# Layernorm, banded attention and a mixture of experts in one kernel: bulk loads issued in ACT's queue, roots by the Sqrt table, k copied out one exponent earlier

## What is computed

```
h   = x + attention(layernorm(x))          # 32 query heads, 8 key/value heads, width 64
out = h + experts(layernorm(h))            # 8 experts, hidden width 1024, top 2, capacity 640

attention: q, k, v = xn @ W_qkv; rotary tables on q and k
           scores = q k^T / 8, -inf where 0 <= q_pos - k_pos < 64
           softmax over the keys and one sink logit per head; times v; @ W_out
layernorm: (x - mean) / sqrt(var + 1e-5)
experts:   gates = softmax(xn2 @ gating_w); top 2; rows scattered to expert slots;
           relu(rows @ w1 + b1) @ w2 + b2; weighted and added back
```

## Time and profile before

| | us |
|---|---|
| median of 3 runs | 1170.53 (1166.02 to 1171.97) |
| the profiled execution, device time | 1165.65 |
| its span in the trace | 1163.8 |
| PE busy in the span | 1047.7 (90%) |
| DVE busy | 891.1 (77%) |
| POOL busy | 709.1 (61%) |
| ACT busy | 642.4 (55%) |

### The profile page before, as it was taken

One profiled execution on the slowest core, in us unless ns is written; L12 is line 12 of the kernel. 1 busy time (PEld: TensorE's weight loads), 2 busy tenths in 40 slices (PEclk: granted clock), 3 DMA queues, 4 the chain that ended last, 5 costly groups with the idle time before them and its releaser, 6 DMA issues. The chain is left out here.

```text
span 1163.8 us, 32636 instructions
## 1 busy us (share of the span) xinstructions
PE 1047.7 (90%) x13260; PEld 760.2 (65%) x13260; DVE 891.1 (77%) x1936; ACT 642.4 (55%) x1597; POOL 709.1 (61%) x586
## 2 busy tenths in 40 slices
PE   4797998998899999989999998999883799999995
PEld 3364665565565666656566665666552799999995
DVE  7999888897898998979999997999973444444442
ACT  2556665565655666565566656656643344444551
POOL 5555565667556686766577675668723266655662
PEclk9898999999999999989999999999996799999998
DMA  3443433343322333232233323233422344344431
GB/s 98 128 124 110 121 107 105 105 114 108 87 75 84 90 93 87 74 103 76 77 111 95 96 75 90 73 88 102 125 68 95 119 100 94 89 109 107 105 103 19
DMA packets 115398, 111.45 MB, mean 96 GB/s; under 512 B 35216, under 2 KB 103888, under 8 KB 115120
## 3 DMA queue, kind: packets, MB, share of 16 engines
q1 hardware_dynamic: 107952, 100.81, 29.6%
q0 software_dynamic: 7296, 8.55, 4.4%
HBM read 74.17 MB, written 21.83 MB: 82 GB/s over the span
## 5 line engine op out<-in xcount | busy, mean ns | idle before, releaser
L778 ACT ACTIVATE probs_ring<-probs_ring,neg_max 128x512 f32<-128x512 f32 x512 | 366.4, 718 | 323.4 <-DVE neg_max L954 322.8
L954 DVE CUSTOM_DVE_ANT_0 probs_ring<-bank,mask,sink_neg 128x512 f32<-128x512 f32 x512 | 361.3, 737 | 62.2 <-PE bank L1276 61.1
L1276 PE MATMUL bank<-qk_st 64*128 64x512 f32 x1024 | 288.4, 640 | 40.3 <-DVE neg_max L954 35.4
L963 DVE STREAM_TRANSPOSE probs_t<-probs_ring 128x1024 f32<-128x1024 f32 x256 | 317.0, 1238 | 0.1
L1297 PE MATMUL bank<-probs_t,v_quads 32*64 32x256 f32 x8192 | 252.4, 384 | 13.6 <-ACT chunk_sb L759 4.7
L1297 PEld LDWEIGHTS bank<-probs_t,v_quads 32*64 32x64 f32 x8192 | 187.5, 133 | 88.1 <-issue 57.7
L646 POOL TENSOR_TENSOR chunk_sb<-chunk_sb,rope_sb 128x512 f32<-128x512 f32 (+1 forms) x94 | 119.9, 1276 | 158.9 <-issue 105.9
L1276 PEld LDWEIGHTS bank<-qk_st 64*128 64x128 f32 x1024 | 86.7, 189 | 110.3 <-DVE neg_max L954 50.8
L651 POOL TENSOR_TENSOR qk_st<-chunk_sb,swap_sb 128x512 f32<-128x512 f32 (+1 forms) x94 | 120.1, 1278 | 7.4
L1326 PEld LDWEIGHTS bank<-wo_sb,heads_sb 64*128 64x128 f32 x992 | 96.9, 189 | 38.3 <-issue 29.8
L647 POOL TENSOR_TENSOR swap_sb<-swap_sb,rope_sb 128x512 f32<-128x512 f32 (+1 forms) x94 | 120.2, 1279 | 0.0
(11 more groups left out here) (144 smaller groups left out, 1527.9 us busy)
## 6 DMA issues: line engine op xcount, KB each, us to landing
v_quads<-v_rows SPq DMA_DIRECT2D x128, 128.0 KB
recip_wide<-recip_rows SPq DMA_DIRECT2D x64, 256.0 KB, 4.5
w_raw<-in_L_ffn_w SPq DMA_DIRECT2D x16, 1024.0 KB, 6.9
swap_sb<-chunk_sb SPq DMA_DIRECT2D x314, 32.0 KB, 3.0
w_raw<-in_L_attn_W_qkv SPq DMA_DIRECT2D x32, 256.0 KB, 2.8
slot_rows<-x2T SPq DMA_DIRECT2D x8, 662.5 KB, 5.2
slots<-slot_rows SPq DMA_DIRECT2D x8, 662.5 KB, 3.9
w_raw<-in_L_attn_W_qkv SPq DMA_DIRECT2D x64, 64.0 KB, 2.6
```

What stands on the lines that cost most here:

```text
L778: nc.scalar.activation(probs[(g * UNITS + n) % RING][:, :], probs[(g * UNITS + n) % RING][:, :], ACT.Exp, bias=neg_max[j][:, n:n + 1], sca ...
L954: nc.vector.tensor_tensor_reduce(probs[(g * UNITS + n) % RING][:, :], SCORE[SCORE_OF[n // 2][n % 2]][:, :], mask[:, L - P - t * P:2 * L - ...
L963: nc.vector.transpose(probs_t[j][:, :, (h // 2) * (2 * P):(h // 2 + 1) * (2 * P)] .rearrange("p b (h q) -> p h b q", h=2)[:, :, :, t * BLK ...
L1276: nc.tensor.matmul(SCORE[SCORE_OF[n // 2][hh]][:, :], qk_st[j][half, h // 2, t * P:(t + 1) * P], qk_st[j][half, PAIRS, :], start=True, sto ...
```

## The change

1. `load_x`, `load_wo` and `zero_rows` are issued by ACT, from `act_ahead`. The loads of sequences 1, 2 and 3 stand at m = 1, 19 and 35, the loads of W_out at n = 8 and the zero fill at n = 13 of periods 0 to 7. They leave SP's list. W_out's loads count on two semaphores in turn.
2. `inverse_root` (Ln, then Exp) becomes `square_root` (Sqrt), and DVE takes a reciprocal ahead of the Newton step. The root of sequences 1 to 3 moves from n = 10 to n = 12 of period 2 and DVE's use of it from n = 11 to n = 15. The roots of the second layernorm move from r = 27 to r = 39, that is to n = 7 of the following period, and DVE's use from r = 28 to r = 43; the four normalisations on ACT move from r = 37, 38, 40, 42 to r = 44 to 47. A small Exp is put behind the first four copies of the start, with its result unused.
3. The copy of chunk KV moves from n = 2 to n = 1, ahead of the exponent of n = 2. The copy of Q01 stays.

```diff
-        CHUNK_OUT_AT = {-14: (KV, Q01), -5: (Q23,)}
+        CHUNK_OUT_AT = {-15: KV, -14: Q01, -5: Q23}
-        VAR_AT, STD_AT, RSTD_AT = 16 + 10, 16 + 11, 16 + 12
+        VAR_AT, STD_AT, RSTD_AT = 16 + 10, 32 + 7, 32 + 11
-        NORM2_AT = {37: 0, 38: 1, 40: 2, 42: 3}
+        NORM2_AT = {44: 0, 45: 1, 46: 2, 47: 3}
-        LATE_VAR_AT, LATE_STD_AT, LATE_RSTD_AT = 2 * UNITS + 10, 2 * UNITS + 10, 2 * UNITS + 11
+        LATE_VAR_AT, LATE_STD_AT, LATE_RSTD_AT = 2 * UNITS + 10, 2 * UNITS + 12, 2 * UNITS + 15
...
             for g in range(GROUPS - 1):
...
                 swap_halves(g + 1, Q23)
-                if g < NKV:
-                    load_wo(g)
-                if g + 2 < B:
-                    load_x(g + 2)
-                if g < E:
-                    zero_rows(g)
...
         @block.scalar
-            def inverse_root(n, tiles):
-
-                nc.scalar.activation(std[:, 0:tiles], var_eps[:, 0:tiles], ACT.Ln).then_inc(s_log, 1)
-                act.wait_ge(s_log, n + 1)
-                nc.scalar.activation(rstd0[:, 0:tiles], std[:, 0:tiles], ACT.Exp, scale=-0.5).then_inc(s_std, 1)
+            def square_root(tiles):
+
+                nc.scalar.activation(std[:, 0:tiles], var_eps[:, 0:tiles], ACT.Sqrt).then_inc(s_std, 1)
...
+            X_LOAD_AT = {1: 1, UNITS + 3: 2, 2 * UNITS + 3: 3}
+
             def act_ahead(m):
+                if m in X_LOAD_AT:
+                    load_x(X_LOAD_AT[m])
+                if m < NKV * UNITS and m % UNITS == 8:
+                    load_wo(m // UNITS)
+                if m < E * UNITS and m % UNITS == 13:
+                    act.wait_ge(s_const, 2)
+                    zero_rows(m // UNITS)
...
         @block.vector
             def rstd_of(n, tiles):
 
                 dve.wait_ge(s_std, n + 1)
+                ln(nc.vector.reciprocal(rstd0[:, 0:tiles], std[:, 0:tiles]))
...
         @block.tensor
-                        pe.wait_ge(s_wo_in, (g + 1) * (16 * PAIRS))
+                        pe.wait_ge(s_wo_in[g % 2], (g // 2 + 1) * (16 * PAIRS))
```

More of the change, by code:

```diff
@@ L129, in moe_layer @@
         s_recip_in = sem("s_recip_in")
-        s_wo_in = sem("s_wo_in")
+        s_wo_in = [sem(f"s_wo_in{i}") for i in range(2)]
         s_sink_in = sem("s_sink_in")
@@ L144, in moe_layer @@
         s_std = sem("s_std")
-        s_log = sem("s_log")
         s_norm = sem("s_norm")
@@ L476, in v_in @@
                                  v_rows.rearrange("(c j) n -> j c n", j=BLK)).then_inc(s_v_in[j], 16)
-            def load_x(b):
-                sp.dma_start(x_sb[:, b * TPB:(b + 1) * TPB, :],
-                             x_rows[:, b * TPB:(b + 1) * TPB, :]).then_inc(s_x_in[b], 16)
-            def load_wo(k):
-                for p in range(PAIRS):
-                    sp.dma_start(wo_sb[p * HD:(p + 1) * HD, 2 * k:2 * k + 2, :],
-                                 w_out.rearrange("(k m d) n -> d k m n", m=QM, d=HD)[:, k, 2 * p:2 * p + 2, :]
-                                 ).then_inc(s_wo_in, 16)
             def recip_out(g):
@@ L771, in act_step @@
                 if n in CHUNK_OUT_AT:
-                    for c in CHUNK_OUT_AT[n]:
-                        chunk_out(g, c)
+                    chunk_out(g, CHUNK_OUT_AT[n])
                 if n == V_NEXT_AT:
@@ L802, in _ @@
                 norm_hi(n)
+            act.wait_ge(s_const, 1)
+            nc.scalar.activation(sink_exp[:, 0:1], identity[:, 0:1], ACT.Exp)
             chunk_out(0, KV)
@@ L806, in _, with load_x, load_wo, zero_rows @@
             chunk_out(0, Q23)
-            def act_ahead(m):
+            def load_x(b):
+                act.dma_start(x_sb[:, b * TPB:(b + 1) * TPB, :],
+                             x_rows[:, b * TPB:(b + 1) * TPB, :]).then_inc(s_x_in[b], 16)
+            def load_wo(k):
+                for p in range(PAIRS):
+                    act.dma_start(wo_sb[p * HD:(p + 1) * HD, 2 * k:2 * k + 2, :],
+                                 w_out.rearrange("(k m d) n -> d k m n", m=QM, d=HD)[:, k, 2 * p:2 * p + 2, :]
+                                 ).then_inc(s_wo_in[k % 2], 16)
+            def zero_rows(e):
+                act.dma_start(slot_rows[e * CAP:(e + 1) * CAP, :].rearrange("(p j) d -> p j d", p=P),
+                             x2T[:, 0:KC + 1, :].rearrange("p c d -> p (c d)")[:, 0:ROW].unsqueeze(1)
+                             .broadcast_to([P, CAP // P, ROW])).then_inc(s_zero_rows, 16)
+            X_LOAD_AT = {1: 1, UNITS + 3: 2, 2 * UNITS + 3: 3}
+            def act_ahead(m):
+                if m in X_LOAD_AT:
[5 more added lines that the diff above has]
+                    zero_rows(m // UNITS)
                 if m == LATE_STD_AT:
@@ L832, in act_route @@
                     act.wait_ge(s_var, b + 3)
-                    inverse_root(b + 2, TPB)
+                    square_root(TPB)
                 if r in X2T_AT:
```

7 lines of the change are left out of this document (1 added, 6 removed).

## The result

| | before | after |
|---|---|---|
| median | 1168.36 us (4 runs, 1166.02 to 1171.97) | 1138.34 us (4 runs, 1135.07 to 1141.75) |
| ratio, 95% interval | | 0.9741 [0.9697, 0.9784] |
| the profiled execution's span | 1163.8 us | 1137.5 us |

What follows compares the result with a forecast made beforehand. It took PE (90% busy) and gaps from delays of PE at n = 3 to 9, of DVE at n = 10 to 3, or shared waits as the bound; terms summed to -12.9, so 1157 us at the median, range 1147 to 1168.

Steps and rivals of the forecast that it cites:

- bulk off SP, with its issues on ACT: Attention, reciprocals' DMA: SP no longer late, -8.0 (ends -8.6, -3.4); 24 issues on ACT, +0.5 (ends 0, +15.5).
- KV's copy: PE's value product loses its 0.29 us wait for the copy in 16 of 31 periods: -4.5 (ends 0, -4.6).
- roots and normalisations: Layernorm roots leave DVE's waits: middle -7.2, late -1.6, start and last -2.5; normalisations at n = 12 to 15 +0.5.
- x just ahead of use: Periods 0, 1 and 2: DVE stalls for late x loads by 3.0, 4.1 and 2.8 us, +9.9 (ends +7.9, +14.1).
- all of the excess: Best end of the bulk term: three late periods take 8.6 us more than 3 x 24.26, all of it saved.
- The other five bulk periods: Periods with bulk DMAs beyond the three late ones: claimed to show no such loss, as far as read.
- The rival that only issue time is saved: Small DMAs' flight stays long; bulk term -3.4, sum -8.3, 1162 us; chance 0.15.
- the 42% of the lower end: Bulk term's smaller end: 1.94 us of issue out of SP's 4.6 us lateness, giving -3.4.
- Each middle wait: DVE's wait at r = 28, three times: 2.6 less a reciprocal of 0.2, -7.2 in all (ends -7.8, -3.0).
- The give-back of 0.5 for the normalisations: Four normalisations on ACT in DVE's stage, n = 12 to 15, three times: +0.5 (ends 0, +6).
- The cover at n = 7: ACT's loads and root (2.8 us) fit before v's copy, needed 1.40 later by Q23: 0; if it fails, +4.2.
- the slower rival: ACT's issues become the bound, delaying v's copy and Q23: sum 0, or 1175 us with x loads later; chance 0.12.

Runs made afterwards that it cites:

- b_xsp: The changed kernel with the three loads of x issued by SP again, far ahead of use; 0.9647 of the kernel before, median 1128.03 us.
- c_mid: The kernel before with all bulk DMAs still issued by SP, but behind the swaps of Q01; ratio 0.9833.
- f_zero: The kernel before with the zero fill alone moved to ACT (n = 13), W_out's loads left on SP; ratio 0.9851, -17.4 us.
- d_fill: The kernel before with three idle matmuls added on PE at n = 14 of periods 9, 17 and 25; ratio 0.9926, 8.6 us faster.
- e_best: The changed kernel with early x loads on ACT, W_out and root at n = 5, normalisations one period on; 0.9662 of the kernel before.
- a_x: The kernel before with the three loads of x alone issued by ACT just ahead of use; ratio 0.9991, -1.1 us.

## Why the prediction was wrong

Forecast and timed, each part alone (the x term as the difference between the changed kernel and b_xsp):

| step | forecast | measured |
|---|---|---|
| bulk off SP, with its issues on ACT | -8.0 + 0.5 | -19.1 (15.6 to 22.6) |
| KV's copy | -4.5 | -3.8 (0.8 to 6.7) |
| roots and normalisations | -7.2 - 1.6 - 2.5 + 0.5 = -10.8 | -15.0 (12.0 to 17.9) |
| x just ahead of use | +9.9 | +11 (+4 to +18) |
| sum | -12.9 | -27; whole change -30.3 |

The parts are no exact sum, since several of them meet in the same waits; the last 3.4 us between -27 and -30.3 lie within the intervals.

**Bulk off SP: this step failed.** It was put as "all of the excess" of three periods at most, -8.6, of which I took -8.0; it measured -19.1, and the traces have 14.5 and 19.8 of it in periods 2 and 5 to 9. That is 11 of the 17 us that the forecast missed. Three things were wrong in it. The excess was taken from one trace, a mild one; the second shows 13.6 in the same periods. "The other five bulk periods show no such loss as far as I read them" was false: period 2 loses 4 us, by x coming late and by POOL's work meeting DVE's Newton step. And what hangs on a late SP was not asked for: behind it stands a late POOL, PE's wait for the split weights and a stretch at the lower clock, which reach into period 9 (1.5 to 1.9 us). The rival that only issue time is saved was far off, and the reading of the Trainium skill (DMA: Bandwidth & Descriptors, "Issuing engines are not separate DMA queues") that was set against the term has to be seen with c_mid: who issues indeed made no difference that can be told, what did was which small DMA stood behind the large one. The sentence on the mechanism ("the zero fill stands five units ahead of the reciprocals and not next to them") was right, and it was the larger half; the 42% of the lower end, by issue time, was refuted by f_zero (and 42% of 8.6 is 3.6, not 3.4). The flight of 2.22 that was taken as the undisturbed one is itself a long one: the writes of the reciprocals in the periods on either side of it take 1.44 and 1.45.

**The roots: right in mechanism, too small.** Each middle wait was charged at its own 2.6 less 0.2. This is what DVE shows: from the `neg_max` of n = 12 to the next it takes 4.29 in period 9 of before and 0.64 with the roots moved, 3.65 less, which is the wait of 2.60 and 1.05 of small operations behind it. These come back as the 1.15 at n = 11 of period 10, so 2.5 is left against the forecast's 2.4. What the term left out is the clock: the pause that the wait makes in PE is followed by a stretch at 1.2 GHz, and d_fill, which fills the pause and leaves the wait, has the three pairs of periods 2.7 and 3.7 shorter. With these the term would be -13.5 to -14.5, within what was measured. The give-back of 0.5 for the normalisations was not seen: e_best moves them away and keeps the 1.15. The cover at n = 7 held: Q23 has no wait for v's copy in these three periods. ACT's timeline of period 10 shows why:

```profile
296.71 1.28 ACT L711 ACT_TABLE_LOAD   x1
...
298.00 0.21 ACT L711 ACTIVATE std<-var_eps 128x4 f32<-128x4 f32 x1
...
298.23 1.28 ACT L749 ACT_TABLE_LOAD   x1
...
299.52 0.72 ACT L749 ACTIVATE probs_ring<-probs_ring,neg_max 128x512 f32<-128x512 f32 x1
```

The pair of loads and the root take 2.81, as forecast, with no room for the drain of the Trainium skill (ScalarE: Activation LUTs, "What ACT_TABLE_LOAD costs"). Why it is not paid here no run shows.

**KV's copy** was right within its interval; the gain per period is 0.37 and not 0.29; I put the other 0.08 down to a pause too short to be listed.

**x** was right in the changed kernel: 10.2 us of waits against 9.9, 3.8, 3.1 and 3.3 for the forecast's 3.0, 4.1 and 2.8. That x alone on ACT cost nothing in the timed runs (a_x) is not explained.

**ACT as issuer**, the slower rival, did not come: W_out's pair takes 1.24 in most periods, but 2.0 to 2.2 in periods 1, 2 and 6, and in period 2 Q23 waited 1.38 for v's copy. Why those three issues took longer is not known.

## What to carry to other kernels

A pause of the engine that bounds the kernel is to be priced with what follows it: look at the granted clock and at the duration of equal matmuls behind the pause before writing down the wait alone. Where a queue runs late, follow it to every engine that it feeds and not only to the wait with its name, and take its cost from more than one trace. What stands in front of a small DMA on the path can cost more by its transfer than by the time of its issue; here moving it to a place where the queue's owner waits anyway was worth as much as moving it to another engine. And work that is moved out of a wait has to be charged where it lands.
